# First guesses of the inverse norms: integer multiply-add on GpSimd and VectorE in the place of two ScalarE activations

## The chip, the cores and the metric

The kernel runs on one core of a Trainium2 chip. A core has a matrix engine (PE, TensorE), a vector engine (DVE, VectorE), a scalar engine (ACT, ScalarE), a general engine (POOL, GpSimd) and a queue engine (SP, SyncE) that here only issues transfers. Each runs an instruction stream of its own, and they meet through semaphores. The metric is the device time of one execution in microseconds (us).

## What is computed

The whole program is a chain of four blocks on an input of 2 x 2048 rows with 128 channels, each block of the form `x = x + layernorm(block(layernorm(x)))`. The fourth block takes more than two thirds of the time, and the change is in it: six layers of windowed attention (16 heads of 64, windows of 32 rows that look one window back) and a gated feed-forward part. What matters of the reference is this:

```python
def l2norm(t):
    return t / jnp.maximum(jnp.linalg.norm(t, axis=-1, keepdims=True), 1e-12)
def attn_layer(x, Wqkv, qs, ksc, Wo):
    q, k, v = jnp.split(x @ Wqkv, 3, -1)          # then split in heads
    q = l2norm(q) * qs
    k = l2norm(k) * ksc
    q = q * cos * scale + rotate_half(q) * sin * scale
    k = k * cos * inv + rotate_half(k) * sin * inv
    return local_attention(q, k, v) @ Wo          # softmax over 64 keys, scale 8
for i in range(6):
    x = attn_layer(shift_tokens(x), Wqkv[i], q_scale[i], k_scale[i], Wo[i]) + x
    x = ffn_layer(shift_tokens(x), ln_g[i], ln_b[i], W1[i], b1[i], W2[i], b2[i]) + x
```

The `l2norm` needs one inverse norm for each row and head, for the query and for the key. The kernel takes the sum of squares, sets a floor of 1e-24 under it, makes a first guess of the inverse root from the bits of the number (a magic constant less half the integer), and improves it by three Newton steps.

## The kernel before

The attention of a layer is cut into units of 128 rows: 16 row tiles of 2 sequences make 32 units. The code of each engine is written out by hand for four units and stands in a loop of eight iterations (`Fori(0, J // 2)`, L1883 on ScalarE, L2038 on VectorE, L1540 on GpSimd, L1686 on TensorE). With six layers the loops' ends jump back 6 x 7 = 42 times. There is no scheduler: each engine does what its body lists, in that order, and waits for semaphores in between. Work on three units overlaps: while unit u is attended, unit u+1 is transposed, and unit u+2 is projected.

For one unit the engines do the following. The names are those of the rows below.

- TensorE: scores of groups 2 and 3 (L1628), transposes of the input tile of u+2 (L1570) and of the key of u+1 (L1592), transposes of the four groups' probabilities (L1638), attention times values (L1652), four projection chunks of u+2 of three matmuls each (L1585 to L1587), scores of groups 0 and 1 of u+1, the query's transposes and the output projection (L1661).
- ScalarE: the exponentials (`exps`, L1841), copies out of the accumulator banks (`drain_v` L1802, `split_x` L1791, `drain_k_T` L1823, `drain_probs` L1849, `drain_attention` L1854, `drain_q_T` L1829 and L1832), squares of the projections (L1797), and two first guesses (L87): `guess`, query, output `d_newton_tmp`, between `drain_v` and `split_x`; `guess_k`, key, output `d_k_root`, behind the fourth group's exponentials.
- VectorE: `sum_squares` of the query (L1955), `floor_sums` (L1974 twice), `normalise` of group 0 (L1999 and L2002), `find_max` of group 2 (L1993), nine Newton steps of the query (L1983, L1985, L1987), `split_x_low` (L1948), `normalise` 1, `find_max` 3, `normalise` 2, `turn` 0 (L1965), `sum_squares` of the key, and so on to `residual` (L2009, L2010).
- GpSimd: floor of the key's sums (L1476), ten Newton steps of the key (L1481 to L1502), scaling of query and key by their inverse norms (L1507), and the rotation's sums (L1470).

The first guess of the query needs `floor_sums` and is needed by VectorE's first Newton step (semaphore `newton`). The first guess of the key needs L1476 and is needed by L1481 (semaphore `k_guess`). The query's inverse norm lets GpSimd scale the query (L1507), which TensorE then transposes.

Of the kernel before, what the change touches and what calls it, by code (L numbers as in the profile page):

```python
# [6 lines left out]
ALU = mybir.AluOpType  # L7
# [5 lines left out]
I32 = mybir.dt.int32  # L13
# [10 lines left out]
RSQRT_MAGIC = 0x5F3759DF  # L24
# [36 lines left out]
RSQRT_STEPS = 11  # L61
# [23 lines left out]
def rsqrt_guess(nc, x, y, offset):  # L85

    return nc.scalar.activation(y.bitcast(I32), x.bitcast(I32), ACT.Identity, scale=-0.5, bias=offset)  # L87
# [1043 lines left out]
K_STEPS = 10  # L1131
# [39 lines left out]
def windowed_transformer(nc, w, x_outer, out):  # L1171

    ctx = ExitStack()
    with ctx:
# [32 lines left out]
        waits_met = m.sem("waits_met")  # L1207
# [90 lines left out]
        XS = U + 2  # L1298
# [98 lines left out]
        with nc.Block() as block:  # L1397
# [53 lines left out]
            def _(pool):  # L1451
# [25 lines left out]

                def newton_k(n, b):

                    pool.wait_ge(k_guess, n + 1)  # L1480
                    nc.gpsimd.tensor_tensor(k_work[:, 0, :], k_sums[:], k_root[:], ALU.mult).then_inc(k_newton, 1)  # L1481
                    pool.wait_ge(k_newton, n * K_STEPS + 1)
                    nc.gpsimd.tensor_tensor(k_work[:, 1, :], k_work[:, 0, :], k_root[:], ALU.mult).then_inc(k_newton, 1)
                    pool.wait_ge(k_newton, n * K_STEPS + 2)
                    pool.sem_inc(waits_met)
                    nc.gpsimd.tensor_scalar(k_work[:, 0, :], k_work[:, 1, :], -10.0 / 3.0, None, ALU.add).then_inc(k_newton, 1)
                    pool.wait_ge(k_newton, n * K_STEPS + 3)
                    nc.gpsimd.tensor_tensor(k_work[:, 2, :], k_work[:, 0, :], k_work[:, 1, :], ALU.mult).then_inc(k_newton, 1)
                    pool.wait_ge(k_newton, n * K_STEPS + 4)
                    pool.sem_inc(waits_met)  # L1490
                    nc.gpsimd.tensor_scalar(k_work[:, 1, :], k_work[:, 2, :], 5.0, None, ALU.add).then_inc(k_newton, 1)
                    pool.wait_ge(k_newton, n * K_STEPS + 5)
                    nc.gpsimd.tensor_tensor(k_work[:, 3, :], k_work[:, 1, :], k_root[:], ALU.mult).then_inc(k_newton, 1)
                    pool.wait_ge(k_newton, n * K_STEPS + 6)
                    nc.gpsimd.tensor_tensor(k_work[:, 0, :], k_sums[:], k_work[:, 3, :], ALU.mult).then_inc(k_newton, 1)
                    pool.wait_ge(k_newton, n * K_STEPS + 7)
                    nc.gpsimd.tensor_tensor(k_work[:, 1, :], k_work[:, 0, :], k_work[:, 3, :], ALU.mult).then_inc(k_newton, 1)
                    pool.wait_ge(k_newton, n * K_STEPS + 8)
                    pool.sem_inc(waits_met)
                    nc.gpsimd.tensor_scalar(k_work[:, 2, :], k_work[:, 1, :], -0.5 / CUBIC ** 3, 1.5 / CUBIC, ALU.mult, ALU.add).then_inc(k_newton, 1)  # L1500
                    pool.wait_ge(k_newton, n * K_STEPS + 9)
                    nc.gpsimd.tensor_tensor(k_inv[:, b, :], k_work[:, 2, :], k_work[:, 3, :], ALU.mult).then_inc(k_newton, 1)  # L1502
# [285 lines left out]
            def _(act):  # L1788
# [13 lines left out]
                    nc.scalar.activation(vals[b][:, jj, (c - 4) * 512:(c - 3) * 512], A[(c + 1) % 2][:], ACT.Copy  # L1802
                                         ).then_inc(v_copied, 1)

                def guess(f):

                    act.wait_ge(floor_set, 2)
                    act.wait_ge(ssq_floor, f * 2 + 1)
                    act.wait_ge(newton, f * RSQRT_STEPS)
                    rsqrt_guess(nc, floored[:], rt[:], guess_offset[:, 0:1]).then_inc(newton, 2)  # L1810

                def guess_k(n):

                    act.wait_ge(floor_set, 2)
                    act.wait_ge(k_floor, n + 1)
                    act.wait_ge(k_newton, n * K_STEPS)
                    rsqrt_guess(nc, k_sums[:], k_root[:], guess_offset[:, 0:1]).then_inc(k_guess, 1)

                def drain_k_T(f, half, b, jj):
                    act.wait_ge(qk_T_ps, f * 4 + (half + 1))  # L1820
                    rows = T0[:].rearrange("p (c t) -> p c t", c=4)
# [41 lines left out]
                with act.Fori(0, DEPTH) as l:  # L1863
                    f0 = l * FRONTS
                    split_x(l * XS)
                    for c in range(4):
                        square(l, 0, c)
                    guess_k(l * XS)
                    drain_v(l, 0, 4, 0, 0)
                    drain_v(l, 0, 5, 0, 0)  # L1870
                    guess(f0)
                    split_x(l * XS + 1)
                    drain_k_T(f0, 0, 0, 0)
                    square(l, 1, 0)
                    drain_k_T(f0, 1, 0, 0)
                    square(l, 1, 1)
                    drain_q_T(f0, 0)
                    square(l, 1, 2)
                    drain_q_T(f0, 1)
                    square(l, 1, 3)  # L1880
                    guess_k(l * XS + 1)
                    exps(l, 0, 0)
                    with act.Fori(0, J // 2) as i:  # L1883
                        for jj in range(2):
                            for b in range(B):
                                u = (i * 2 + jj) * 2 + b
                                a = l * U + u
                                f1 = f0 + (u + 1)
                                b1, jj1 = 1 - b, (jj + b) % 2
                                exps(l, u, 1)  # L1890
                                drain_v(l, u + 1, 4, b1, jj1)
                                drain_v(l, u + 1, 5, b1, jj1)
                                guess(f1)
                                split_x(l * XS + (u + 2))
                                drain_k_T(f1, 0, b1, jj1)
                                drain_probs(a, 0)
                                exps(l, u, 2)
                                drain_attention(a, 0)
                                drain_k_T(f1, 1, b1, jj1)
                                square(l, u + 2, 0)  # L1900
                                drain_probs(a, 1)
                                square(l, u + 2, 1)
                                drain_q_T(f1, 0)
                                exps(l, u, 3)
                                guess_k(l * XS + (u + 2))
                                drain_probs(a, 2)
                                drain_attention(a, 1)
                                square(l, u + 2, 2)
                                drain_probs(a, 3)
                                drain_attention(a, 2)  # L1910
                                square(l, u + 2, 3)
                                drain_attention(a, 3)
                                exps(l, u + 1, 0)
                                drain_q_T(f1, 1)

                    def split_group(mg):
                        act.wait_ge(f_xT_ps, mg + 1)
                        nc.scalar.activation(fx, T0[:], ACT.Identity, scale=vecs[:, 0:1], bias=vecs[:, 1:2]).then_inc(f_xT, 1)
                        act.wait_ge(f_xT, mg + 1)
                        nc.scalar.activation(fxh[:], fx, ACT.Copy).then_inc(f_xh, 1)  # L1920

                    act.wait_ge(small_dma, (l + 1) * (MLP_LOADS * DMA))
                    m0 = l * (GROUPS + 1)
                    split_group(m0)

                    act.wait_ge(f_xh, m0 + 1)
                    nc.scalar.activation(table_probe[:], fx[0:1, 0:1], ACT.Gelu).then_inc(probed, 1)
                    with act.Fori(0, GROUPS) as g:
                        q = l * GROUPS + g
                        for c, (o, sz) in enumerate(FF_CHUNKS):  # L1930
                            act.wait_ge(f_gate_ps, q * 3 + (c + 1))
                            if c == 0:

                                act.wait_ge(f_act, q * 3 + 3)
                            if c == 2:
                                act.wait_ge(f_act, q * 3 + 4)
                            nc.scalar.activation(gl[0:sz, c % 2, :], S[c % 2][0:sz, :], ACT.Gelu,
                                                 bias=vecs[0:sz, 5 + c:6 + c]).then_inc(f_gelu, 1)

                        act.wait_ge(f_a_ps, q * 3 + 3)  # L1940
                        split_group(m0 + g + 1)
# [3 lines left out]
            def _(v):  # L1945
# [30 lines left out]
                def newton_steps(f, b):  # L1976

                    out_sb = rn[:, b, :]
                    v.wait_ge(ssq_floor, f * 2 + 2)
                    for i in range(3):  # L1980
                        sums, step, root = (sums_ps, step_ps, rt[:]) if i == 0 else (floored[:], rt2[:], root_ps)
                        v.wait_ge(newton, f * RSQRT_STEPS + (3 * i + 2))
# [328 lines left out]
```

## Time and profile before

| | us |
|---|---|
| three runs | 5954.01, 5956.59, 5966.02 (median 5956.59) |
| profiled execution, device time | 5959.97 |
| its span in the trace | 5958.0 |
| busy: DVE, ACT, POOL | 4327.4 (73%), 3775.4 (63%), 2536.1 (43%) |
| exponentials L1841 on ACT, 3096 | 1008.4 |
| first guesses L87 on ACT, 198 of the query and 204 of the key | 66.0 and 64.4 |

The span is what lies between the first and the last instruction in the trace. A row of a timeline gives the start, the duration, the engine, the line, the operation with output and input, and in brackets how long the engine was idle just before and what released it; "issue" means that nothing which the profile shows was waited for. Where several instructions of a line follow each other they stand in one row with their number. The TensorE clock is given as a share of its full speed.

### The profile page before, as it was taken

How to read it: one execution, taken by the hardware profiler on the slowest of the kernel's cores; microseconds unless marked ns; L12 is line 12 of the kernel's file. 1: busy time of each engine (PE TensorE's matmuls, PEld its weight loads, DVE VectorE, ACT ScalarE, POOL GpSimd, SP SyncE). 2: the span in 40 equal slices, each digit the busy share in tenths (PEclk: the TensorE clock that was granted, in tenths of full speed). 3: DMA queues.
4: the chain of work that ended last, by engine and by line, in shares of the span. 5: the costliest groups of instructions: out<-in, count | busy, mean ns of one | idle time of the engine just before them, and what ended most of it. 6: DMA issues, size and time to landing. Idle time of an engine off the chain costs nothing. (4 is left out here: it accounts for less than half of the span.)

```text
span 5958.0 us, 148484 instructions
## 1 busy us (share of the span) xinstructions
PE 5089.0 (85%) x41656; PEld 4226.5 (71%) x41656; DVE 4327.4 (73%) x11808; ACT 3775.4 (63%) x12267; POOL 2536.1 (43%) x3943
## 2 busy tenths in 40 slices
PE   5987868997089996999869998799987999689994
PEld 3665767986078874888758886588866888578883
DVE  4454575776578886788868888688886888778887
ACT  1112433342089983899749996599956999389982
POOL 0000000000266662666626665466645666266661
PEclk7786887998599997999989998899988999899997
DMA  0000110000111111011101111111111111111111
GB/s 19 0 0 14 44 27 1 0 0 1 43 24 26 23 30 39 22 25 26 47 20 24 27 23 45 24 24 24 26 43 25 26 23 24 46 24 23 26 25 49
DMA packets 103769, 146.50 MB, mean 25 GB/s; under 512 B 65414, under 2 KB 72859, under 8 KB 103131
## 3 DMA queue, kind: packets, MB, share of 16 engines
q1 hardware_dynamic: 94155, 109.63, 8.1%
q0 software_dynamic: 9232, 33.12, 1.7%
q14 instruction: 307, 2.51, 0.1%
q8 instruction: 75, 1.23, 0.1%
HBM read 49.13 MB, written 2.10 MB: 9 GB/s over the span
## 5 line engine op out<-in xcount | busy, mean ns | idle before, releaser
L1841 ACT ACTIVATE d_probs<-d_S_ps,d_neg_max 128x96 f32<-128x96 f32 x3096 | 1008.4, 342 | 69.3 <-issue 57.7
L1470 POOL TENSOR_TENSOR d_qk<-d_qk,d_sin_terms 128x512 f32<-128x512 f32 x792 | 989.3, 1271 | 14.1 <-DVE d_sin_terms L1965 14.1
L1628 PEld LDWEIGHTS d_S_ps<-d_kT,d_q_blocks 128*128 128x128 f32 x6240 | 806.7, 193 | 2.5
L1628 PE MATMUL d_S_ps<-d_kT,d_q_blocks 128*128 128x96 f32 x6240 | 805.3, 272 | 0.0
L1965 DVE TENSOR_TENSOR d_qk<-d_A_ps,d_tables 128x512 f32<-128x512 f32 x816 | 560.2, 686 | 218.1 <-ACT d_squares L1797 146.9
L1841 ACT ACTIVATION_READ_ACCUMULATOR d_probs<-d_S_ps,d_neg_max 128x1 f32 x3096 | 644.8, 208 | 0.0
L1585 PE MATMUL d_A_ps<-d_wqkv_hi,d_xT_hi 128*128 128x512 f32 x1212 | 586.1, 484 | 17.3 <-DVE d_sin_terms L1965 12.3
L1797 ACT ACTIVATE d_squares<-d_A_ps 128x512 f32<-128x512 f32 x816 | 491.7, 603 | 133.9 <-PE d_A_ps L1587 133.6
L1965 DVE TENSOR_TENSOR d_sin_terms<-d_A_ps,d_tables 128x512 f32<-128x512 f32 x816 | 554.7, 680 | 0.0
L1592 PE MATMUL d_T_ps<-d_ident,d_qk 128*128 128x128 f32 x3168 | 501.3, 282 | 50.4 <-POOL d_qk L1507 45.2
L1849 ACT ACTIVATE d_probsT<-d_PT_ps 96x512 f32<-96x512 f32 (+1 forms) x768 | 460.3, 599 | 70.3 <-PE d_PT_ps L1638 69.8
L1955 DVE TENSOR_REDUCE d_sum_squares<-d_squares 128x16 f32<-128x1024 f32 x402 | 486.8, 1211 | 18.5 <-issue 17.9
L1587 PE MATMUL d_A_ps<-d_wqkv_lo,d_xT_hi 128*128 128x512 f32 x1212 | 487.4, 402 | 0.0
L1586 PE MATMUL d_A_ps<-d_wqkv_hi,d_xT_lo 128*128 128x512 f32 x1212 | 486.0, 401 | 0.0
L1638 PE MATMUL d_PT_ps<-d_ident,d_probs 128*96 128x128 f32 (+1 forms) x3072 | 464.6, 274 | 0.0
L1507 POOL TENSOR_TENSOR d_qk<-d_qk,d_inv_norm 128x1024 f32<-128x1024 f32 x198 | 376.8, 1903 | 182.6 <-DVE d_inv_norm L1987 182.2
L1592 PEld LDWEIGHTS d_T_ps<-d_ident,d_qk 128*128 128x128 f32 x3168 | 363.0, 144 | 121.6 <-issue 50.2
L2002 DVE TENSOR_TENSOR d_probs<-d_probs,d_PT_ps 128x384 f32<-128x384 f32 x768 | 425.3, 554 | 26.5
L1993 DVE TENSOR_REDUCE d_neg_max<-d_S_ps 128x4 f32<-128x384 f32 x780 | 427.4, 548 | 14.0 <-PE d_S_ps L1628 14.0
L1661 PE MATMUL d_PT_ps<-d_wo,d_attnT 128*128 128x128 f32 x3072 | 393.0, 281 | 0.0
L1661 PEld LDWEIGHTS d_PT_ps<-d_wo,d_attnT 128*128 128x128 f32 x3072 | 357.3, 191 | 40.9 <-issue 40.9
L1507 POOL TENSOR_TENSOR d_qk<-d_qk,d_k_inv_norm 128x1024 f32<-128x1024 f32 x198 | 377.0, 1904 | 15.1
(404 smaller groups left out, 11227.0 us busy)
## 6 DMA issues: line engine op xcount, KB each, us to landing
d_v_early<-d_v SPq DMA_DIRECT2D x198, 256.0 KB, 3.0
d_v_early<-d_v SPq DMA_DIRECT2D x198, 128.0 KB, 2.3
d_tables<-L_ffn_rotary POOLq DMA_DIRECT2D x7, 2048.0 KB, 9.7
d_qk<-L_ffn_Wqkv POOLq DMA_DIRECT2D x21, 512.0 KB, 4.1
d_xs<-d_xb SPq DMA_DIRECT2D x96, 63.5 KB
d_xs<-d_xb SPq DMA_DIRECT2D x48, 127.0 KB
ax_fp_blocks<-L_ffn_blocks_gu SPq DMA_DIRECT2D x16, 256.0 KB, 3.8
ax_fp_scales<-L_ffn_scales_gu SPq DMA_DIRECT2D x64, 64.0 KB, 3.3
```

Of the source, the lines that this page charges most:

```text
L1470: nc.gpsimd.tensor_tensor(c4[:, :, s, :], c4[:, :, s, :], s4[:, :, 1 - s, :], ALU.add).then_inc(rotated, 1)
L1507: nc.gpsimd.tensor_tensor(r3, r3, inverse.unsqueeze(2).broadcast_to([P, HEADS, HD]), ALU.mult).then_inc(scaled, 1)
L1585: nc.tensor.matmul(bank[:], xh[:], wh[:, sl], start=True, stop=False)
L1586: nc.tensor.matmul(bank[:], xl[:], wh[:, sl], start=False, stop=False)
L1587: nc.tensor.matmul(bank[:], xh[:], wl[:, sl], start=False, stop=True).then_inc(proj_ps, 1)
L1592: last = nc.tensor.transpose(T0[:, p * P:(p + 1) * P], raw[:, k, col:col + P], ident[:])
L1628: last = nc.tensor.matmul(S[g % 2][:, n * SEEN:(n + 1) * SEEN], qx[:, p, half, :], kT[b][jj][:, p, HALF * half:HALF * half + SEEN], start= ...
L1661: last = nc.tensor.matmul(Y[:, 0:D], oT[:, p, :], wo[:, p, :], start=(p == 0), stop=(p == 7))
L1797: nc.scalar.activation(sq[:, k, half * 512:half * 512 + 512], A[(c + 1) % 2][:], ACT.Square).then_inc(proj_squared, 1)
L1841: nc.scalar.activation(pr[:, g, n, seen_columns(g)], S[g % 2][:, n * SEEN:(n + 1) * SEEN], ACT.Exp, bias=nmax[:, g, n:n + 1], accum_out=de ...
L1955: nc.vector.tensor_reduce(ssq[:, k, :, 0], sq[:, k, :].rearrange("p (h d) -> p h d", d=HD), AX.X, ALU.add).then_inc(ssq_ready, 1)
L1965: nc.vector.tensor_tensor(terms[:, k, cols].rearrange("p (h d) -> p h d", d=HD), A[(c + 1) % 2][:].rearrange("p (h d) -> p h d", d=HD), ta ...
```

## The change

Each first guess moves to the engine that runs the Newton steps behind it. For the key, GpSimd does one `tensor_scalar` on integers: the bits of the sum times -0.5 plus the magic constant. For the query VectorE does the same. The two helper functions of ScalarE and all their calls go, and with them `rsqrt_guess` is no longer called there. The semaphores stay: GpSimd itself now sets `k_guess`, and VectorE itself adds the 2 to `newton`.

```diff
                 def newton_k(n, b):
 
+                    pool.wait_ge(k_floor, n + 1)
+                    pool.sem_inc(waits_met)
+                    nc.gpsimd.tensor_scalar(k_root[:].bitcast(I32), k_sums[:].bitcast(I32), -0.5, float(RSQRT_MAGIC),
+                                            ALU.mult, ALU.add).then_inc(k_guess, 1)
                     pool.wait_ge(k_guess, n + 1)
                     nc.gpsimd.tensor_tensor(k_work[:, 0, :], k_sums[:], k_root[:], ALU.mult).then_inc(k_newton, 1)
...
-                def guess(f):
-
-                    act.wait_ge(floor_set, 2)
-                    act.wait_ge(ssq_floor, f * 2 + 1)
-                    act.wait_ge(newton, f * RSQRT_STEPS)
-                    rsqrt_guess(nc, floored[:], rt[:], guess_offset[:, 0:1]).then_inc(newton, 2)
-
-                def guess_k(n):
-
-                    act.wait_ge(floor_set, 2)
-                    act.wait_ge(k_floor, n + 1)
-                    act.wait_ge(k_newton, n * K_STEPS)
-                    rsqrt_guess(nc, k_sums[:], k_root[:], guess_offset[:, 0:1]).then_inc(k_guess, 1)
-
...
-                                guess(f1)
                                 split_x(l * XS + (u + 2))
                                 drain_k_T(f1, 0, b1, jj1)
                                 drain_probs(a, 0)
...
                                 exps(l, u, 3)
-                                guess_k(l * XS + (u + 2))
                                 drain_probs(a, 2)
...
                     v.wait_ge(ssq_floor, f * 2 + 2)
+                    v.sem_inc(waits_met)
+                    nc.vector.tensor_scalar(rt[:].bitcast(I32), sums_ps.bitcast(I32), -0.5, float(RSQRT_MAGIC), ALU.mult, ALU.add
+                                            ).then_inc(newton, 2)
                     for i in range(3):
```

Below are pieces of the engines' instruction orders. An ISA or REGISTER_ALU row is a semaphore or register instruction. First ScalarE, in the first unit of the loop body, from the copies of the value projection on, in the kernel before:

```order
L1801 ISA
L1802 ACTIVATE d_v<-d_A_ps 128x512
L1808 ISA
L1809 REGISTER_ALU
L87 ACTIVATE d_newton_tmp<-d_sums_floored,d_guess_offset 128x16
L1790 ISA
L1791 ACTIVATE d_xT_hi<-d_A_ps 128x128
```

The same place in the changed kernel:

```order
L1805 ISA
L1806 ACTIVATE d_v<-d_A_ps 128x512
L1794 ISA
L1795 ACTIVATE d_xT_hi<-d_A_ps 128x128
L1810 ISA
```

The guess and its two waiting instructions are gone, and the copy of the transposed input follows the value's copies at once. Next VectorE, in the first unit of the loop body, around the maximum of group 2 (L1993) and the first Newton step (L1983), in the kernel before:

```order
L1992 ISA
L1993 TENSOR_REDUCE d_neg_max<-d_S_ps 128x4
L1979 ISA
L1982 ISA
L1983 TENSOR_TENSOR d_PT_ps<-d_PT_ps,d_newton_tmp 128x16
```

And in the changed kernel:

```order
L1980 ISA
L1981 TENSOR_REDUCE d_neg_max<-d_S_ps 128x4
L1964 ISA
L1966 TENSOR_SCALAR d_newton_tmp<-d_PT_ps 128x16
L1970 ISA
L1971 TENSOR_TENSOR d_PT_ps<-d_PT_ps,d_newton_tmp 128x16
```

One instruction that computes stands ahead of the Newton steps. On GpSimd the integer multiply-add likewise stands between L1476 and the key's first Newton step. TensorE's and SP's instructions are the same in both.

The compiled programs have 64 bytes for every instruction, semaphore and register instructions included. Counted in them from the start of each engine's stream, the attention loop's body, which ends with the jump back, is:

| engine | before: first to last (number) | changed: first to last (number) |
|---|---|---|
| ScalarE | 582 to 948 (367) | 572 to 910 (339) |
| VectorE | 1943 to 2231 (289) | 1945 to 2241 (297) |
| GpSimd | 327 to 493 (167) | 331 to 505 (175) |
| TensorE | 1494 in number | the same |

## Rows read from the trace of the kernel before

**Rows 1.** The page: busy time, share and instructions of each engine.

```profile
PE 5089.0 (85%) x41656; PEld 4226.5 (71%) x41656; DVE 4327.4 (73%) x11808; ACT 3775.4 (63%) x12267; POOL 2536.1 (43%) x3943
```

**Rows 2.** Busy time by stretch: two attention units; columns PE, PEld, DVE, ACT, POOL, clock.

```profile
4004.60:4021.90 17.30, 17.30 (x168) 14.62 (x169) 14.23 (x37) 16.11 (x59) 11.22 (x19) 1.00 0.10 23
4021.90:4040.30 18.40, 17.40 (x168) 14.52 (x168) 14.33 (x36) 15.93 (x58) 11.71 (x19) 1.00 0.12 26
```

**Rows 3.** Timeline of TensorE just behind a jump back of the loops.

```profile
4025.18 1.03 PE L1628 MATMUL d_S_ps<-d_kT,d_q_blocks 128*128 128x96 f32 x8
4027.21 0.33 PE L1570 MATMUL d_A_ps<-d_ident,d_x_tile 128*128 128x128 f32 x1 [1.00 <-ACT d_v L1802]
4027.51 0.63 PE L1592 MATMUL d_T_ps<-d_ident,d_qk 128*128 128x128 f32 x4
4027.98 0.60 PE L1638 MATMUL d_PT_ps<-d_ident,d_probs 128*96 128x128 f32 x4
...
4030.58 0.50 PE L1585 MATMUL d_A_ps<-d_wqkv_hi,d_xT_hi 128*128 128x512 f32 x1
```

**Rows 4.** Timeline of ScalarE at the same jump back.

```profile
4023.36 0.59 ACT L1832 ACTIVATE d_q_blocks<-d_T_ps 64x512 f32<-64x512 f32 x1
4025.27 0.34 ACT L1841 ACTIVATE d_probs<-d_S_ps,d_neg_max 128x96 f32<-128x96 f32 x1 [1.31 <-issue]
```

**Rows 5.** Timeline of VectorE at the same jump back.

```profile
4024.71 1.22 DVE L1955 TENSOR_REDUCE d_sum_squares<-d_squares 128x16 f32<-128x1024 f32 x1 [0.41 <-issue]
...
4026.37 0.55 DVE L2002 TENSOR_TENSOR d_probs<-d_probs,d_PT_ps 128x384 f32<-128x384 f32 x1
4026.85 0.55 DVE L1993 TENSOR_REDUCE d_neg_max<-d_S_ps 128x4 f32<-128x384 f32 x1
4027.87 0.18 DVE L1983 TENSOR_TENSOR d_PT_ps<-d_PT_ps,d_newton_tmp 128x16 f32<-128x16 f32 x1 [0.47 <-ACT d_newton_tmp L87]
...
4029.71 0.29 DVE L1948 TENSOR_TENSOR d_xT_lo<-d_A_ps,d_xT_hi 128x128 fp32r<-128x128 f32 x1
```

**Rows 6.** Timeline of VectorE, then TensorE, in the unit without a jump.

```profile
4011.38 0.29 DVE L1948 TENSOR_TENSOR d_xT_lo<-d_A_ps,d_xT_hi 128x128 fp32r<-128x128 f32 x1
...
4012.04 0.50 PE L1585 MATMUL d_A_ps<-d_wqkv_hi,d_xT_hi 128*128 128x512 f32 x1
```

**Rows 7.** Waits of the whole span: us in total, times, longest.

```profile
POOL d_k_sums L1476 <- DVE d_sum_squares L1955: 661.0, 204, 6.2
POOL d_k_work L1481 <- ACT d_k_root L87: 176.7, 204, 2.1
ACT d_probs L1841 <- issue: 57.7, 42, 1.6
```

**Rows 8.** Groups by line and shape: busy us, mean ns, idle before.

```profile
L1486 POOL TENSOR_SCALAR d_k_work<-d_k_work 128x16 f32<-128x16 f32 x204 | 53.5, 262 | 39.8 <-POOL d_k_work L1483 39.8
...
L70 DVE TENSOR_SCALAR d_ff_rstd<-d_ff_ve 128x4 int32<-128x4 int32 x60 | 11.4, 190 | 2.1
```

**Rows 9.** The page, transfers of instructions: packets, MB, share of 16 engines.

```profile
q14 instruction: 307, 2.51, 0.1%
```

**Rows 10.** Transfers in 3952:4022.3, one iteration of four units.

```profile
q14 instruction: 5, 0.04, 0.2%
```

**Rows 11.** Transfers in 4022.6:4022.9, behind ScalarE's jump back.

```profile
q14 instruction: 1, 0.01, 7.2%
```

**Rows 12.** Transfers in 2944.6:2945.2, a layer's last iteration, near ScalarE's loop end.

```profile
q14 instruction: 1, 0.01, 4.4%
```

**Rows 13.** Transfers in 2947.3:2947.8, behind VectorE's loop end.

```profile
q14 instruction: 1, 0.01, 5.9%
```

**Rows 14.** Timeline of VectorE, first work behind its loop's end.

```profile
2947.01 0.87 DVE L2070 BATCH_NORM_STATS2 d_ff_stats<-d_xs 128x6 f32<-128x128 f32 x4 [0.53 <-issue]
```

**Rows 15.** Busy time of TensorE by stretch, feed-forward part; then clock, DMA share.

```profile
5104.30:5107.86 3.56, 3.54 (x8) 0.50 0.30 112
5108.20:5109.58 1.38, 1.38 (x7) 1.00 0.03 6
5114.90:5118.30 3.40, 0.17 (x2) 0.50 0.22 92
```

**Rows 16.** Timeline of TensorE in the same part.

```profile
5112.64 0.46 PE L1755 MATMUL d_PT_ps<-d_ff_xT_hi,d_w_hi 128*85 128x512 f32 x1 [2.90 <-DVE d_sin_terms L2101]
```

More of the change, by code:

```diff
@@ L1867, in _ @@
                         square(l, 0, c)
-                    guess_k(l * XS)
                     drain_v(l, 0, 4, 0, 0)
                     drain_v(l, 0, 5, 0, 0)
-                    guess(f0)
                     split_x(l * XS + 1)
@@ L1880, in _ @@
                     square(l, 1, 3)
-                    guess_k(l * XS + 1)
                     exps(l, 0, 0)
```

## The prediction, made before the changed kernel ran

> **What bounds the kernel now.** I read the page first: TensorE is busy 85% of the span, no other engine more than 73% [rows 1]. Then the stretches between successive input transposes in the attention loop. An ordinary unit takes 17.30 us, of which TensorE is busy 17.30, at the full granted clock (1.00, its 2.4 GHz level). The unit behind a jump back takes 18.40 with 17.40 busy [rows 2]. So three units of four are bound by TensorE alone, and what the fourth takes longer, 1.1 us, is an idle TensorE. The timelines show where: TensorE waits 1.00 us for ScalarE's `drain_v` [rows 3], because ScalarE starts its first exponentials 1.31 us after its last work, with nothing that it waits for [rows 4]. The waits list this 42 times, 57.7 us in all [rows 7], once for each jump back. VectorE has only 0.41 us of it [rows 5].
>
> What ScalarE does there is fetch its own program. The transfers of instructions are 8.2 KB each (2.51 MB in 307) [rows 9], 128 instructions of 64 bytes. One iteration has five of them [rows 10], and one lies just behind ScalarE's jump back [rows 11]; ScalarE starts 2.4 to 2.7 us after that window. My reading: an engine holds four blocks of 128, fetches the next one on entering a block, and throws the oldest away. Where are the edges? In a layer's last iteration one transfer comes just as ScalarE issues the last instructions of its loop [rows 12] and one just behind VectorE's loop end, by VectorE's first work there [rows 13, 14]. Matched to the counts of the compiled programs, ScalarE has edges at 561, 689, 817 and 945, and VectorE at 1979, 2107 and one between 2232 and 2237, say 2235. ScalarE's body, 582 to 948, touches four blocks and calls for a fifth: five don't fit, each is fetched anew in each iteration, and that is the five of rows 10. VectorE's body, 1943 to 2231, touches three and calls for a fourth, which fit: no stall.
>
> **The change, part by part.** Durations are from the profiled execution (5959.97 us, its span 5958.0), 3.4 us above the median of 5956.59; I give the sum against it and take the 3.4 off at the end.
>
> ScalarE loses two guesses per unit. In an ordinary unit this is worth nothing: TensorE has no idle time there [rows 2]. GpSimd gains one instruction per unit, and its wait for ScalarE goes: 176.7 us over 204 keys, 0.87 each [rows 7]. An integer `tensor_scalar` of 128x16 on GpSimd is not in the trace; its float form takes 0.26 with 0.20 of waiting [rows 8]. Bounds: 0.2 to 0.9, and even the upper leaves the chain where it was; GpSimd waits 3.2 us per key for VectorE anyway (661.0 over 204) [rows 7]. 0 us.
>
> VectorE gains one instruction in the query's chain. The integer `tensor_scalar` of 128x4 takes 0.19 [rows 8], so +0.21 with the issue. In the ordinary unit VectorE doesn't wait for the guess; the lower half of the transposed input is then ready at 4011.67 + 0.21 = 4011.88, and TensorE needs it at 4012.04 [rows 6]. Hidden, by 0.16. If the hand-over takes that up, up to 0.1 us in each of some 150 ordinary units: 0 to +15 us. I take 0.
>
> The last part is where the instructions lie. ScalarE's body becomes 572 to 910: it no longer enters the block at 945, so it needs four blocks and its stall goes. VectorE's body becomes 1945 to 2241: it now runs over 2235, six instructions ahead of its jump back, as ScalarE's ran over 945 three ahead. It touches four blocks and calls for a fifth, and its head is no longer there at the jump. I expect the stall to change engine. What is that worth in one of the 42?
>
> - VectorE jumps back right behind `residual`, with no queue of work to hide the fetch, where ScalarE still had some (its last work starts at 4023.36, behind the transfer [rows 4, 11]). From ScalarE, the whole fetch is 2.4 us (last moment of rows 11 to 4025.27) to 3.0; I take 2.9. VectorE has 0.3 of a jump's cost already, so `sum_squares` starts 2.64 us later, at 4027.35 instead of 4024.71 [rows 5]; bounds 2.1 to 2.8.
> - TensorE then waits for the probabilities of group 0: VectorE's L2002 ended at 4026.92, now 4029.56. TensorE transposed them at 4027.98 [rows 3]. It has L1570 and the key's transposes to do until then, earlier than before since ScalarE isn't late, and is idle some 2.7 us.
> - `find_max` ends at 4030.04 (4026.85 + 0.55 + 2.64), the guess takes 0.21 and the nine steps 1.84 (4027.87 to 4029.71) [rows 5], so `split_x_low` starts at 4032.09 and gives its result at 4032.4, which TensorE's L1585 of the next unit but one waits for. Before it ran at 4030.58 [rows 3]: 1.85 later. The way over the probabilities gives 4029.65 + 2.60 = 4032.25, 1.7 later. I take 1.9 with the hand-over; bounds 1.4 to 2.2.
> - The idle 1.00 of TensorE by ScalarE is not taken off again: the 1.9 is counted from rows that hold it.
>
> 42 x 1.9 = +80 us (59 to 92).
>
> Then the clock. At a jump TensorE now idles 2.7 us instead of 1.00, and with 1.00 the stretch kept its full level [rows 2]. In the feed-forward part the granted clock is 0.50 (the 1.2 GHz level) behind an idle time of 2.90 us and another wait [rows 15, 16], and 8 matmuls of 512 columns take 3.56 us at 0.50 where 7 take 1.38 at 1.00 [rows 15]. One such stretch of 3.6 us of work at half level loses 1.8 us. If it came at each jump, 42 x 1.8 = +76; if never, 0. No row shows a single idle time of 2.7 us inside dense work in this loop. I take half, +38.
>
> Sum: 80 + 38 = +118 us on 5959.97, so 6078; less the 3.4 of this execution, about 6075. Its own range is 6015 (59 and no clock) to 6125 (92 and 76).
>
> The Trainium skill (Runtime: NRT & Kernel Launch, section Instruction fetch mechanics) has the same mechanism with other sizes: the instruction memory is a FIFO of 512 instructions in two blocks of 256, and a taken branch to something outside them waits for a transfer. The trace here has transfers of 128, and agrees in the total. With blocks of 256 every second of my edges would be one; ScalarE's stall says 689 and 945. If 2235 is one of VectorE's, the forecast stands, and if 2107 is, VectorE's body stays in two blocks and has no stall.
>
> **The rivals.**
>
> 1. ScalarE's stall goes and VectorE gets none (edges or the number of blocks held are not what I think). For it: VectorE's edge is placed by one transfer and a distance of a few instructions [rows 13, 14], and the new body runs over it by seven only. Against: ScalarE's ran over its own by four, and stalled 42 times. Then the unit behind a jump costs 17.3 instead of 18.4: 42 x 1.1 = -46, 5911 us.
> 2. The stall is not one of code, or both bodies keep what they had: 5957 us, up to 5972 with VectorE's 0.1 us. For it: the five transfers aren't tied to an engine by any row. Against: the time and number of ScalarE's stalls fit no semaphore.
> 3. Slower in another way: no stall moves to VectorE, but its 0.21 us is not hidden and shows in each of the 192 units: +40, less 46 if ScalarE's goes. It decides when `split_x_low` comes later than TensorE at L1585, and there are 0.37 us (4011.67 to 4012.04) for 0.21 [rows 6]. 5950 to 5995 us.
> 4. VectorE stalls, and so does ScalarE still: the two lie beside each other, and VectorE's comes last; as the forecast, within 10 us.
>
> **Chances.** Forecast with rival 4: 0.82. Rival 1: 0.10. Rival 2: 0.05. Rival 3: 0.03. The predicted time is the likeliest case's 6075. The range reaches down to 5950 (half of what is left lies below it) and up to 6125. This kernel's measurement can tell a change of about 0.2%, 12 us, from none. Faster by more: rival 1 and a little of 3, 0.11. Within: 0.06. Slower: 0.83.
>
> **What the changed profile would show.** Right: the wait of ScalarE's L1841 on "issue" is gone; VectorE's `sum_squares` at the loop's head has a wait on "issue" of about 3 us, 42 times, some 120 us in all; still about five transfers of instructions per iteration; the unit behind a jump takes 20.3 us, or more where the clock falls, and ordinary units 17.3; in the unit behind a jump TensorE waits for VectorE's probabilities and for `split_x_low`. The granted clock in the attention loop is below 1.00 behind the jumps if the clock term is right, and TensorE's whole busy time grows. Wrong: VectorE's wait stays at 0.4 us (rival 1, with no transfers in the loop), or ScalarE's stays (rival 2), or ordinary units take 17.5 (rival 3).

## The result and the profile after

The changed kernel takes 6107.73 us (median of four runs, 6091.09 to 6110.86) against 5961.31 of the kernel before beside it: a ratio of 1.0237, 95% interval 1.0209 to 1.0265. The forecast was 6075, its range 5950 to 6125. The profiled execution took 6110.86 with a span of 6109.0, 151 more than before.

Two lines of the page of the changed kernel, then two of its waits, whole span. The waits give us in total, times and longest; all answer to [rows 1, 7, 9].

```profile
PE 5177.8 (85%) x41656; PEld 4288.3 (70%) x41656; DVE 4354.9 (71%) x12006; ACT 3737.5 (61%) x11865; POOL 2579.1 (42%) x4147
...
q14 instruction: 303, 2.48, 0.1%
```

```profile
DVE d_sum_squares L1940 <- issue: 125.9, 42, 3.2
...
PE d_PT_ps L1642 <- DVE d_probs L1990: 114.1, 42, 2.9
```

ScalarE's 42 waits on issue are gone, VectorE has 42 of 3.0 us each, and TensorE waits 42 times, 2.7 us each, for what VectorE does behind them. TensorE runs the same 41656 matmuls and is busy 89 us longer. The transfers of instructions on this queue are nearly as many as before (303 to 307), but another engine asks for them. Behind the jump back that is shown below, one lies in 4111.3:4111.8, while VectorE stands (from 4110.57 to 4113.49); before the change one lay likewise behind ScalarE's jump [rows 11].

```profile
q14 instruction: 1, 0.01, 6.4%
```

The timeline of one jump back, in the order of [rows 4, 5, 3]: ScalarE, then VectorE, then TensorE.

```profile
4110.24 0.34 ACT L1831 ACTIVATE d_probs<-d_S_ps,d_neg_max 128x96 f32<-128x96 f32 x1
...
4110.34 0.23 DVE L1998 TENSOR_TENSOR d_xb<-d_PT_ps,d_xb 128x64 f32 x1
4113.49 1.22 DVE L1940 TENSOR_REDUCE d_sum_squares<-d_squares 128x16 f32<-128x1024 f32 x1 [2.94 <-issue]
...
4115.16 0.55 DVE L1990 TENSOR_TENSOR d_probs<-d_probs,d_PT_ps 128x384 f32<-128x384 f32 x1
4115.63 0.55 DVE L1981 TENSOR_REDUCE d_neg_max<-d_S_ps 128x4 f32<-128x384 f32 x1
4116.10 0.17 DVE L1966 TENSOR_SCALAR d_newton_tmp<-d_PT_ps 128x16 int32<-128x16 int32 x1
4116.30 0.18 DVE L1971 TENSOR_TENSOR d_PT_ps<-d_PT_ps,d_newton_tmp 128x16 f32<-128x16 f32 x1
...
4118.32 0.29 DVE L1933 TENSOR_TENSOR d_xT_lo<-d_A_ps,d_xT_hi 128x128 fp32r<-128x128 f32 x1
...
4112.49 0.63 PE L1596 MATMUL d_T_ps<-d_ident,d_qk 128*128 128x128 f32 x4
4115.77 0.64 PE L1642 MATMUL d_PT_ps<-d_ident,d_probs 128*96 128x128 f32 x4 [2.66 <-DVE d_probs L1990]
```

Here ScalarE goes on at once. VectorE ends its residual at 4110.57 and starts 2.9 us later. TensorE has done its transposes by 4113.1 and waits 2.66 us until the probabilities come.

The stretches from one transpose of the input tile (L1574) to the next, columns as in [rows 2]: three units behind a jump, then an ordinary one.

```profile
4261.11:4281.51 20.40, 17.50 (x170) 14.53 (x168) 16.15 (x42) 16.21 (x56) 12.04 (x20) 1.00 0.10 23
3371.47:3393.07 21.60, 18.97 (x169) 15.83 (x168) 16.14 (x42) 16.20 (x56) 12.02 (x20) 0.92 0.10 22
3296.41:3319.62 23.21, 20.58 (x169) 17.05 (x168) 16.24 (x42) 16.40 (x56) 12.43 (x21) 0.85 0.09 20
4087.70:4105.00 17.30, 17.30 (x170) 14.57 (x168) 14.40 (x39) 15.79 (x55) 11.82 (x20) 1.00 0.10 23
```

TensorE now idles behind the transpose of the input tile where it idled ahead of it, so the long stretch is the next one by this division; it is counted here as the unit behind the jump. The 42 are of three kinds. In 6 the granted clock stays at 1.00 and they take 20.4 to 20.6 us; in 17 it is about 0.92 over the unit (21.6 to 21.9 us); in 19 about 0.85 (22.9 to 23.5 us). Their mean is 22.20, where the long stretches' was 18.48. TensorE's busy time in them is 17.5, 19.0 and 20.5 us on average, for the same matmuls. The account of the 151 us: 42 x (20.45 - 18.48) = 83 by waiting (20.45 is the mean of the six undisturbed), 42 x (22.20 - 20.45) = 73 by the clock, the other units of the attention loop 13 less, the rest of the program 8 more. Of the 13, 5 belong to the stretch just ahead of the long one (17.26 in place of 17.38 us), so that the two stretches at a jump, taken together, price the waiting at 1.85 us a jump, 78 in all.

### The profile page after: what moved, and what is told of

Read it like the earlier page. It is cut to its first block and busy times, and to the rows that moved or that the text cites. A ratio compares the mean times of both kernels' runs of the same rounds, so it can differ in the third digit from the quotient of the medians.

```text
span 6109.0 us, 147884 instructions
## 1 busy us (share of the span) xinstructions
PE 5177.8 (85%) x41656; PEld 4288.3 (70%) x41656; DVE 4354.9 (71%) x12006; ACT 3737.5 (61%) x11865; POOL 2579.1 (42%) x4147
## 5 line engine op out<-in xcount | busy, mean ns | idle before, releaser
L1632 PEld LDWEIGHTS d_S_ps<-d_kT,d_q_blocks 128*128 128x128 f32 x6240 | 826.9, 197 | 3.2
L1632 PE MATMUL d_S_ps<-d_kT,d_q_blocks 128*128 128x96 f32 x6240 | 825.9, 277 | 0.0
L1589 PE MATMUL d_A_ps<-d_wqkv_hi,d_xT_hi 128*128 128x512 f32 x1212 | 595.4, 491 | 20.6 <-DVE d_sin_terms L1950 13.4
L1642 PE MATMUL d_PT_ps<-d_ident,d_probs 128*96 128x128 f32 (+1 forms) x3072 | 477.0, 279 | 114.1 <-DVE d_probs L1990 114.1
L1596 PE MATMUL d_T_ps<-d_ident,d_qk 128*128 128x128 f32 x3168 | 518.5, 289 | 48.4 <-POOL d_qk L1511 43.6
L1642 PEld LDWEIGHTS d_PT_ps<-d_ident,d_probs 128*96 128x96 f32 (+1 forms) x3072 | 361.3, 139 | 157.9 <-DVE d_probs L1990 124.1
```

The source lines that it names most:

```text
L1589: nc.tensor.matmul(bank[:], xh[:], wh[:, sl], start=True, stop=False)
L1596: last = nc.tensor.transpose(T0[:, p * P:(p + 1) * P], raw[:, k, col:col + P], ident[:])
L1632: last = nc.tensor.matmul(S[g % 2][:, n * SEEN:(n + 1) * SEEN], qx[:, p, half, :], kT[b][jj][:, p, HALF * half:HALF * half + SEEN], start= ...
L1642: last = nc.tensor.transpose(PT[0][0:rows, n * P:(n + 1) * P], pr[:, g, n, 0:rows], ident[:])
```

## The experiments

Theory P: an engine holds four blocks of 128 instructions, so a loop that needs more than four fetches its head again at each jump back, and the change moved VectorE's loop over an edge and ScalarE's away from one. Rival Q: the guess on VectorE makes its chain late. The kernel before took about 5974 us beside these runs (the expectations were worked out from 5957), so the ratios count.

### Only VectorE's code moved (changed kernel)

```diff
+                for _ in range(40):
+                    v.sem_inc(waits_met)
                 with v.Fori(0, DEPTH) as l:
```

> The changed kernel, with 40 semaphore increments that nobody waits for ahead of VectorE's layer loop, once in the program: its attention loop body (297 instructions) moves from 1945..2241 to 1985..2281, so that by my count it touches the blocks at 1979, 2107 and 2235 and calls for 2363: four. Theory of blocks (P): no wait on issue at VectorE's loop head (0.4 us at most in place of 3), none at ScalarE's, jump units at 17.3 to 17.5 us in place of 22.2, full granted clock in the loop: 5911 us (5900 to 5925). Rival (Q), that the guess on VectorE is what makes its chain late: nothing changes, 6105 us.

5925.65 us against 5973.66, ratio 0.9922 (0.9905 to 0.9938); P's 5911 to 5957 is 0.9923. VectorE's waits on issue at the loop's head are

```profile
DVE d_sum_squares L1940 <- issue: 19.1, 42, 0.5
```

and one iteration has no transfer of instructions at all; the two stretches at a jump are nearly ordinary ones (before: 18.4 and 17.4; changed: 17.3 and 22.2):

```profile
3980.13:3997.38 17.25, 17.25 (x169) 14.51 (x168) 13.95 (x35) 15.79 (x56) 11.42 (x20) 1.00 0.10 23
3997.38:4015.14 17.76, 17.51 (x169) 14.52 (x168) 14.86 (x41) 16.10 (x56) 12.08 (x20) 1.00 0.12 26
```

Forty instructions that run once and do nothing turn a kernel 2.4% slower than before into one 0.8% faster. With the guess still on VectorE, Q is out as the cause of the loss.

### Each half of the change alone

Key: the added lines of `newton_k`, and `guess_k` with its calls taken out. Query: the added lines of `newton_steps`, and `guess` with its calls taken out.

> Only the key's guess moves to GpSimd; the query's stays on ScalarE. ScalarE's body becomes 576..930 (355), short of the edge at 945; VectorE's is as before (1943..2231). P: ScalarE's stall goes and VectorE gets none: 5911 us (5900 to 5925), the 42 jump units at 17.3. Q: the key's guess is off the path, so as before, 5957 us.

5915.41 us, ratio 0.9902 (0.9885 to 0.9918). P's direction, and about 12 us better than its number (part of it is found below). Its median is the lowest of all kernels run, though the interval overlaps that of ScalarE's shift alone (0.9895 to 0.9930).

> Only the query's guess moves to VectorE; the key's stays on ScalarE. ScalarE 578..928, no stall; VectorE 1945..2241 (297) as in the changed kernel, over the edge at 2235. P: 6105 us (6085 to 6120), 42 waits on issue of about 3 us at VectorE's loop head. Q says the same, so this run with the key's alone splits the change, and doesn't tell P from Q.

6123.14 us, ratio 1.0250 (1.0233 to 1.0267), as expected (6105 to 5957 is 1.0248). VectorE's waits on issue are 42, 125.7 us in all. The whole loss sits in the query's half, and by the run with VectorE's code moved it isn't in the arithmetic.

### The changed arithmetic with the stall put back on ScalarE

```diff
+                for _ in range(40):
+                    act.sem_inc(waits_met)
                 with act.Fori(0, DEPTH) as l:
...
+                for _ in range(40):
+                    v.sem_inc(waits_met)
                 with v.Fori(0, DEPTH) as l:
```

> The changed kernel with VectorE shifted by 40 as in the run with VectorE alone shifted, and ScalarE's body shifted by 40 semaphore increments ahead of its layer loop, to 612..950, over the edge at 945. P: ScalarE stalls at each jump as before the change (42 waits on issue of 1.3 us), VectorE doesn't: the time before, 5957 us (5950 to 5970), with all of the change's arithmetic in it. Q: 6105.

5960.45 us, ratio 0.9978 (0.9965 to 0.9991), the time of the kernel before but for 0.2%, with both guesses moved. Its waits:

```profile
ACT d_probs L1831 <- issue: 54.4, 42, 1.5
DVE d_sum_squares L1942 <- issue: 19.1, 42, 0.5
```

### The kernel before, its code moved and nothing else

With 112 increments ahead of ScalarE's layer loop:

> The kernel before, with 112 semaphore increments ahead of ScalarE's layer loop: its body of 367 moves to 694..1060, touches the blocks at 689, 817 and 945 and calls for 1073: four. P: its 42 waits on issue of 1.37 us go, with both guesses still on ScalarE: 5911 us (5900 to 5930; the 112 increments run once, while ScalarE waits). Q: 5957.

5919.6 us, ratio 0.9913 (0.9895 to 0.9930); P's number is 0.9923. ScalarE has no wait on issue in the loop. Most of what the key's half gains can be had without changing an operation.

With 10 increments ahead of VectorE's:

> The kernel before, with 10 semaphore increments ahead of VectorE's layer loop: its body (289 instructions, unchanged) moves to 1953..2241 and runs over the edge that I put at 2235. No guess has moved. P (blocks of code): VectorE stalls about 3 us at each of 42 jumps, ScalarE too beside it; 6100 us (6080 to 6120). Q (the guess on VectorE makes the loss): 5957 us.

6074.74 us against 5974.8, ratio 1.0171 (1.0154 to 1.0188), under the expected 1.0240. VectorE's stall came as expected, beside ScalarE's, and the transfers of one iteration (4037:4110) doubled:

```profile
DVE d_sum_squares L1955 <- issue: 127.7, 42, 3.2
ACT d_probs L1841 <- issue: 58.1, 42, 1.6
```

```profile
q14 instruction: 10, 0.08, 0.4%
```

The loss is 100 us and not 143. The clock fell behind only 15 of the 42 jumps, where it fell behind 36 in the changed kernel. Here TensorE idles twice, 1.07 us for ScalarE and then 1.40 for VectorE, instead of once for 2.7. That the halving of the idle time is what kept the clock up was not tested by itself; the shifts by 2 and 5 below bear on it.

### Where the edge is, and what a jump right behind it costs

The same with 2, 5 and 24 increments. Single runs, beside a kernel before of 5974 us.

> The kernel before, with 2 semaphore increments ahead of VectorE's layer loop: its body ends at 2233. The edge lies behind 2231 and at or ahead of 2237 by my reading, most likely at 2235. P with the edge at 2234 or later: 5957 us; with the edge at 2232 or 2233: 6100 us. I expect 5957 (two in three).

6166.44 us: a miss of both numbers, 5957 and 6100. It stalls already, so the edge is at 2232 or 2233 and not at 2235, and each stall takes 4.0 us, not 3.0.

> The kernel before with VectorE's body shifted by 5, to 1948..2236. From the shift by 2 the edge is at 2232 or 2233. There the jump back stood at most one instruction behind it and VectorE's wait on issue was 4.0 us each (166.6 us in all); with the shift by 10 it stood eight or nine behind it, ahead of the wait for the output projection, and the wait was 3.0. Theory: a jump right behind an edge queues its transfer behind the one that fetches ahead, so that only what stands between edge and jump hides the first. The last six instructions are the residual's two additions and the jump, behind that wait. Expected with the edge three or four ahead of the jump: near 4.0 us each (3.6 to 4.0), 6160 us (6120 to 6170). Rival, that each stalled jump costs 3.0 and the shift by 2 was a slower execution: 3.0 us each and 6075 us.

6152.36 us, inside its range, but 3.5 us each, a little under the expected 3.6 to 4.0. The direction is the theory's, and the rival (3.0 us, 6075) fails.

> The kernel before with VectorE's body shifted by 24, to 1967..2255: the edge at 2232 or 2233 is 22 or 23 instructions ahead of the jump, and the body still touches four blocks and calls for a fifth. Five blocks don't fit wherever the edges are: 42 waits on issue of 3.0 us (not 4.0), 6075 us (6060 to 6110). If instead only an edge right ahead of the jump stalls, it is 5960.

6146.38 us. The stall is the expected 3.05 us, the time isn't: 71 us more than 6075, or 54 when both are set against their kernel before. The waits of the three in this order:

```profile
DVE d_sum_squares L1955 <- issue: 166.6, 42, 4.1
```

```profile
DVE d_sum_squares L1955 <- issue: 148.1, 42, 3.7
```

```profile
DVE d_sum_squares L1955 <- issue: 128.2, 42, 3.2
```

The last one's timeline of VectorE shows why its time is still high:

```profile
4436.70 0.18 DVE L1999 RECIPROCAL d_PT_ps<-d_den 128x4 f32<-128x4 f32 x1
4437.48 0.56 DVE L2002 TENSOR_TENSOR d_probs<-d_probs,d_PT_ps 128x384 f32<-128x384 f32 x1 [0.60 <-DVE d_PT_ps L1999]
```

In the kernel shifted by 10 these two follow each other within 0.21 us. Here the body starts at 1967 and the next edge is some ten instructions on (128 ahead of 2232 or 2233), and VectorE stands a second time, 0.60 us here and 0.53 on average, at about the place where that block is due. TensorE's wait grows from 1.40 to 1.92 us a jump, and the clock falls behind 35 jumps.

The second stop is in all 48 iterations, the first of each layer too. The kernels shifted by 10 and by 2 have a smaller one at other places, and the waits of the kernel before have none. In the order of shifts 24, 10 and 2:

```profile
DVE d_probs L2002 <- DVE d_PT_ps L1999: 25.4, 48, 0.7
```

```profile
DVE d_probs L2002 <- DVE d_PT_ps L1999: 13.8, 48, 0.3
```

```profile
DVE d_xT_lo L1948 <- issue: 11.2, 42, 0.3
```

Counted in the traces from the `sum_squares` at the head of the loop, semaphore instructions included, the stops are 7, 150 and 30 instructions on. With the bodies' starts at 1967, 1953 and 1945 that makes 1974, 2103 and 1975: the stop stays at the same place of the stream while the code moves under it, or stands one block of 128 further on. So it goes with the block's edge and with no instruction.

### Is it the clock that makes the rest?

```diff
+                    for p in [0, 1, 2, 3] * again:
+                        nc.tensor.transpose(T0[:, p * P:(p + 1) * P], raw[:, 1, p * P:(p + 1) * P], ident[:])
                     transpose_four(1, half)
...
-                                transpose_k(f1, 0)
+                                transpose_k(f1, 0, 4 if jj == 0 and b == 0 else 0)
```

> The changed kernel; in the first of the loop's four units TensorE does the key's four transposes of half 0 four times more, ahead of the real ones, into the same bank (16 matmuls, 1.9 us), in the time in which it else waits for VectorE's probabilities. The result is the same, VectorE's stall stays. If the part of the loss above 20.4 us per jump unit comes by the granted clock, TensorE has under 1 us of idle time there, the clock stays at 1.00 and all jump units take 20.4 to 20.6 us: 42 x 1.75 = 74 less than 6108, plus 6 x 1.9 in the layers' first units: about 6045 us (6030 to 6060). If it comes by something else, 6105 or more.

6046.92 us against 5974.8, ratio 1.0123 (1.0106 to 1.0140); 6045 to 5957 is 1.0148. VectorE's stall is untouched and TensorE's wait for it is 0.9 us in place of 2.7. The waits, and then a unit behind a jump, with 16 matmuls more in it:

```profile
DVE d_sum_squares L1942 <- issue: 125.5, 42, 3.2
...
PE d_PT_ps L1644 <- DVE d_probs L1992: 39.4, 42, 1.1
```

```profile
4061.06:4081.73 20.67, 19.27 (x185) 16.24 (x184) 16.15 (x42) 16.22 (x56) 12.09 (x20) 1.00 0.10 23
```

The units behind a jump take 20.5 us on average and the clock is 1.00 in them. Against the changed kernel (1.0237), more work made it 1% faster: the difference of 1.7 us a jump between 20.5 and 22.2 was the clock's.

## Why the prediction was right, and where a size was off

- ScalarE's stall goes: right. None of its 42 is left, and 42 x 1.1 us, 46 in all, is about what the three kernels without any stall gain (ratios 0.9922, 0.9902 and 0.9913, for a worked-out 0.9923).
- VectorE gets one of 2.9 us: right, `sum_squares` waited 2.94 us on issue in the jump shown, 126 us in all where "some 120" stood. The edge was put at 2235 and is at 2232 or 2233; it made no difference to the forecast, since the new body ends at 2241, and that is luck of the distance: a body that ended at 2233 or 2234 would have been called wrongly, as the run with the shift by 2 was.
- TensorE's price of that stall, 1.9 us a jump, 80 us in all: measured on the six undisturbed units 1.97, and 83 (1.85 and 78 with the stretch ahead of each). Both ways of the prediction are in it: in each of the six TensorE waits 2.6 to 2.8 us for the probabilities, 1.7 more than it idled before, and then 0.27 to 0.29 more for `split_x_low`. Where the clock fell, TensorE comes to that place so late that the second wait is gone.
- The guesses' own cost, put at 0: 0.17 us on VectorE and 0.20 with 0.19 of waiting on GpSimd, where the prediction had 0.19 and up to 0.46:

```profile
L1482 POOL TENSOR_SCALAR d_k_root<-d_k_sums 128x16 int32<-128x16 int32 x204 | 41.4, 203 | 38.8 <-POOL d_k_sums L1476 38.8
...
L1966 DVE TENSOR_SCALAR d_newton_tmp<-d_PT_ps 128x16 int32<-128x16 int32 x198 | 32.7, 165 | 0.9 <-DVE d_PT_ps L1959 0.9
```

  This "0" is two small things that nearly cancel where neither engine stalls. With the key's guess on GpSimd the first unit of each layer takes 26.4 us on average and not 28.1, in every run that has it there: 10 us. With the query's guess on VectorE the second stretch at a jump takes 17.77 us, and 17.61 without (both halves shifted clear of the edge against the key's half alone): 8 us if it holds in all 48 iterations. I had looked for neither place. With ScalarE's stall in place the 8 us don't show: that stretch takes 17.39 us, and 17.38 in the kernel before.
- The clock term was mis-sized: +38, half of its bound of 76, for want of a row with an idle time of 2.7 us inside dense work. It was 73. The clock fell behind 36 of 42 jumps and cost 1.2 us in 17 of them and 2.8 in 19, 2.0 on average where 1.8 was estimated from the feed-forward rows. So "I take half" is the step that was off, and the half by chance, not by a row; the upper end was nearly the value. The 35 us that it was short are the whole of the 33 between the forecast's +118 and the 151 of the profiled executions; the other terms cancel.
- Rival 4 had both stalls beside each other cost as much as VectorE's alone, within 10 us. ScalarE's was gone, so it didn't come up; but the shift by 10 has both, and its ratio is 1.0171 against the changed kernel's 1.0237, some 40 us less.
- The block's size: the shifts of VectorE's body by 2, 5, 10 and 24 all stall and by 0 none, and the changed body stalls at a shift of 0 and not of 40. That fits four blocks of 128. The traces also show the size by itself. In the kernel before, ScalarE's transfers in mid-iteration come one at a time, in 4044.7:4044.9 and in 4069.6:4069.8, with none in 4045:4069.5:

```profile
q14 instruction: 1, 0.01, 16.8%
```

```profile
q14 instruction: 1, 0.01, 9.7%
```

  They are 24.9 us apart in an iteration of 70.4, and 128 of 367 instructions are that share; blocks of 256 would be twice as far apart. The stops of VectorE at 1974 or 1975 and at 2103 say the same. The Trainium skill (Runtime: NRT & Kernel Launch, section Instruction fetch mechanics) gives blocks of 256 instructions, two of them held. On this queue the measurement disagrees with the size and agrees with the total of 512, which the stalls fit. The page of the profile has a second queue of instructions with 75 transfers of 16.4 KB (256 instructions) in every run; it is the same in all of them, and no run here shows what its blocks do at a jump.

## What to carry to other kernels

When a wait on "issue" comes back once per loop iteration, count the instructions of the engine's loop body, semaphore instructions included, and look at the transfers of instructions: here a body that spans more than four 128-instruction blocks, the one fetched ahead included, cost VectorE 3.0 to 4.0 us of idle time at each jump back, and ScalarE 1.4. An edit that adds eight instructions can cross that edge and an edit elsewhere can uncross it, so a small change in time after a small edit should first be tested with idle instructions ahead of the loop. And if TensorE is the bound, price a new idle time of some 2.5 us also with what the clock takes behind it, which here was nearly as much again (73 us beside 83).

## What was not expected of the hardware

A jump back at most one instruction behind an edge stalls 4.0 us, three or four behind it 3.5, eight or more behind it 3.0 (means of 42; the first two and the one of the shift by 24 from single runs). The transfer that was called for on entering the last block may stand in the way of the one for the head; no run separates the two.

What lowers the clock isn't the length of one idle time alone. An idle time of 2.5 us cut in two pieces (1.07 and 1.40) lowered it behind 15 of 42 jumps, one of 2.7 behind 36, one of 2.4 (the query's half alone) behind 38, and one of 0.9 behind none. But 1.07 and 1.92 (the shift by 24) lowered it behind 35, and 1.07 with 2.2 or 2.3 (the shifts by 5 and 2) behind all 42. Which of the 42 are spared stays open.
